# Sixteen filler-row transfers, placed behind the row loads of the third turn of tiles in place of in front of them

## The reference

```
probs = softmax(xf @ gate_w.T)                 # 4096 tokens, 16 experts
top_w, top_idx = top_k(probs, 4)               # 4 experts for each token, weights scaled to sum 1
act  = silu(xf @ w1[e].T) * (xf @ w3[e].T)     # hidden size 128
moe_out = sum over the token's 4 experts of weight * (act @ w2[e].T)
x = layernorm(x + moe_out + shared(x))
```

## Time and profile before

| | |
|---|---|
| median of 3 runs | 611.17 us |
| lowest, highest | 606.96, 620.32 us |
| the profiled execution | 603.63 us |
| its span (first to last instruction) | 601.8 us |
| PE, DVE, ACT, POOL busy | 86%, 75%, 61%, 58% of the span |
| first row load of the second half | 303.56 us |
| the sixteen pads on SP | 318.86 to 336.0 us |
| mean granted TensorE clock | 0.95 of full speed |

### The profile page before, as it was taken

The page is one execution under the profiler, slowest core; times in us unless marked ns, Lnnn a source line. Parts: engine busy times, 40 slices in busy tenths (PEclk is TensorE's granted clock), DMA queues, the critical chain, the costliest instruction groups (busy, mean ns, idle before and its releaser), DMA issues.

```text
span 601.8 us, 11085 instructions
## 1 busy us (share of the span) xinstructions
PE 518.6 (86%) x3184; PEld 450.2 (75%) x3184; DVE 448.6 (75%) x1053; ACT 369.8 (61%) x844; POOL 346.3 (58%) x320
## 2 busy tenths in 40 slices
PE   5997999999998999887597789989898999889752
PEld 2786878787877878775466688889897888888641
DVE  5868899999899989998896434444456877867544
ACT  4735585868586858751653445666575676775535
POOL 0331223868687786757788556565656666657520
PEclk9998999999999999998789589899999999999778
DMA  7999645978596857579967655555559998987873
GB/s 244 200 224 341 92 115 118 286 206 209 132 207 172 162 180 172 134 180 298 325 190 226 177 177 152 150 174 157 164 170 295 312 315 277 324 287 270 277 281 138
DMA packets 79006, 128.07 MB, mean 213 GB/s; under 512 B 10358, under 2 KB 57911, under 8 KB 78650
## 3 DMA queue, kind: packets, MB, share of 16 engines
q1 hardware_dynamic: 42714, 61.21, 36.3%
q0 software_dynamic: 28688, 58.35, 34.6%
q10 hardware_dynamic: 7552, 7.88, 3.8%
HBM read 75.89 MB, written 47.35 MB: 205 GB/s over the span
## 4 chain that ended last, share of the span: by engine, by line
PE 43%; DVE 25%; ACT 10%; issue 9%; another core or an unknown queue 5%; DMA 3%; SPq 3%; POOL 2%; ACTq 0%; DVEq 0%; POOLq 0%
PE bank L811 6%; PE bank L1028 6%; PE bank L1030 6%; PE bank L1029 5%; PE bank L833 4%; PE bank L1077 4%; PE bank L865 3%; PE bank L947 2%; ACT ty L1310 2%; SPq L535 2%; DVE x1c L1426 2%; PE bank L985 2%; DVE vc L1426 2%; ACT xtT_hi L1295 2%
## 5 line engine op out<-in xcount | busy, mean ns | idle before, releaser
L778 POOL DMA_INDIRECT token_parts<-ty,goes x144 | 141.0, 979 | 94.6 <-issue 32.7
L749 POOL DMA_INDIRECT expert_rows<-row,slot x112 | 128.8, 1150 | 60.9 <-issue 33.9
L1028 PE MATMUL bank<-w_hi,xtT_hi 128*128 x288 | 89.7, 311 | 9.2 <-DVE xtT_lo L1785 7.3
L1029 PE MATMUL bank<-w_lo,xtT_hi 128*128 x288 | 84.0, 292 | 1.6 <-issue 1.6
L1030 PE MATMUL bank<-w_hi,xtT_lo 128*128 x288 | 82.7, 287 | 0.7 <-issue 0.7
L1785 DVE TENSOR_TENSOR xtT_lo<-bank,xtT_hi 128x512 fp32r<-128x512 f32 x72 | 49.5, 688 | 23.7 <-issue 12.1
L1028 PEld LDWEIGHTS bank<-w_hi,xtT_hi 128*128 128x128 f32 x288 | 56.6, 197 | 13.7 <-issue 13.4
L1770 DVE TENSOR_TENSOR taT_lo<-bank,taT_hi 128x256 fp32r<-128x256 f32 x72 | 30.3, 420 | 47.0 <-issue 23.8
L1310 ACT ACTIVATE ty<-bank,tail 128x256 f32<-128x256 f32 x144 | 62.0, 495 | 0.0
L1288 ACT ACTIVATE tsl<-bank 128x256 f32<-128x256 f32 x72 | 29.4, 408 | 51.3 <-remote 34.9
L1295 ACT CAST xtT_hi<-bank 128x512 fp32r<-128x512 f32 x72 | 43.4, 602 | 24.9 <-remote 16.0
(11 more groups left out here) (229 smaller groups left out, 1342.2 us busy)
## 6 DMA issues: line engine op xcount, KB each, us to landing
xt<-expert_rows SPq DMA_DIRECT2D x144, 129.0 KB
row<-token_parts SPq DMA_DIRECT2D x18, 640.0 KB
xT<-in_xT SPq DMA_DIRECT2D x8, 512.0 KB
xtok<-in_b_out SPq DMA_DIRECT2D x8, 512.0 KB
xtok<-in_x POOLq DMA_DIRECT2D x8, 512.0 KB
x<-taps POOLq DMA_DIRECT2D x8, 512.0 KB
x<-ups POOLq DMA_DIRECT2D x8, 512.0 KB
w_hi<-in_w POOLq DMA_DIRECT2D x1, 4096.0 KB, 16.9
```

Source lines behind the costliest of these rows:

```text
L749: pool.indirect_dma_start(out=rows_d, out_offset=bass.IndirectOffsetOnAxis(ap=slot[q][:, n:n + 1], axis=0), in_=src[:, n // TOPK, n % TOPK ...
L778: pool.indirect_dma_start(out=parts_d, out_offset=bass.IndirectOffsetOnAxis(ap=goes[:, q_ * UNROLL + u:q_ * UNROLL + u + 1].bitcast(U32), ...
L1028: te_.matmul(ps, x_hi, w_hi, start=first, stop=False)
L1029: te_.matmul(ps, x_hi, w_lo, start=False, stop=False)
```

## The change

In `between`, the call of `pads()` moves from after the turn with number 1 to after the turn with number 2. Nothing is added or removed.

```diff
             def between(g):
-                if g == 1:
+                if g == 2:
                     pads()
-                if g == 2:
                     table_row(1)
                 if g == TFULL - 1:
```

## The result

The changed kernel takes **617.87 us** as the median of 6 runs (615.0 to 626.83), beside 610.7 us for the kernel before in 6 runs (606.96 to 620.32). By medians that is 7.2 us more; the ratio is 1.0161 with a 95% interval of 1.0114 to 1.0208, or 9.8 us. So the change made the kernel slower, by 1.2% in the medians and 1.6% in the ratio. The forecast, 607.4 us, has the wrong sign, and the time lies 0.9 us above the upper end of the range.

What follows compares the result with a forecast made beforehand. SP's loads standing behind the pads were taken as the bound, with PE's pace after pair 12. The hole moves to pair 12 and shrinks 3.8 us: 603.6 to 599.8 profiled, plus 7.5 gives a 607.4 us median; range 602 to 617.

Steps and rivals of the forecast that it cites:

- The case that the effect is absorbed later: Rival, chance 0.10: a later wait that does not move absorbs the gain; the time stays at 611.2 us.
- the halt moves with the pads: Main case, chance 0.42: PE's and ACT's halt follows the pads; pair 12 at 352.7, a gain of 3.8 us.
- tail copied at 328.5: Main case's time for pair 7's tail copy, with pair 7's transposes at 327.15; pair 11's loads issued by 329.5.
- The text's own sign: ACT's long wait before a silu: 330 to 347 if the halt moves with the pads, 324 to 332 if it stays.
- the halt stays and the hole grows: Rival, chance 0.32: halt not tied to the pads; pair 12 at 356.5 to 361.7, loss 0 to 5.2 us, 613.8 us.
- block with its register loads: SP's sixteen pads with two register loads: bounds 12.9 us (pads 0.70 us apart) and 18.01 us (as profiled before).
- table and register load: On SP, the table transfers and the register load behind them, up to the first row load: 1.94 us.
- load to transposes: From SP's issue of the first row load to PE's transposes, including the landing of 2.57 us: 3.28 us.
- The threshold of this rival: The loss decides once SP issues the block later than 333.3; that needs pair 7's tail copied after 332.3.
- the costs at nothing: Pad writes beside POOL's scatters, and the wait for `padded` behind the fourth turn (2.57 us if uncovered), were put at nothing.
- The rival without a halt: Rival, chance 0.12: pads run 0.70 us apart, block 12.9 us, pair 12 at 347.6; 8.9 us less, 602.3 us.
- theory A: From the experiments: the halt stays between pairs 7 and 8, delaying pair 7's tail copy and everything behind pair 11's loads.

Runs made afterwards that it cites:

- fit_b: Pads dealt out on SP: five behind pair 5's loads, one each behind 6's and 7's, nine behind 9's; 618.59 us, ratio 0.9942 to the kernel before.
- e_first: All sixteen pads behind pair 3's loads, on the chip without halts; 559.5 us, ratio 0.9998 to the kernel before.
- e_after_again: The changed order (sixteen pads behind pair 11's loads) built again, on the chip without halts; 560.56 us, ratio 1.0013 to the kernel before.
- before_again: The kernel before, unchanged, run again on a second chip with halts; 618.54 us, ratio 1.0046 to the kernel before.
- a hold of PE: PE repeats the transposes of pair 6's first tile forty times; 630.3 us in the kernel before, 627.46 us in the changed kernel.

## Why the prediction was wrong

**What bounds the kernel: right.** A loss ahead of pair 12 reached the end one to one (9.1 us at pair 12, 9.0 at the last pair), at the forecast pace of 3.3 us a pair. The case that the effect is absorbed later did not come.

**The step that failed: the choice between the two cases.** The prediction put two terms side by side, with pair 12 at 352.7 or at 356.5 to 361.7, and chose the first, "the halt moves with the pads". The reason given was the coincidence, the 8.58 us lying inside the block and the other waits of the kind being at most 4.8 us. In the changed kernel PE halts between pair 7 and pair 8 with no pad issued. On the clock of before, ACT's long wait is at 333.0 to 339.6 and the first pad at 342.4. So the term "tail copied at 328.5" became 340.6, and pair 12 came at 365.6 instead of 352.7. The text's own sign, ACT's long wait between 330 and 347 for the first case and at 324 to 332 for the second, would have named the wrong case: the wait had moved to a later silu, but not with the pads. What did go with the pads is the 8.58 us at the one silu, as the profiles above show. A coincidence in one trace weighed more than it could bear: the four shorter waits without pads had already shown that pads are not needed. The Trainium skill (Runtime: NRT & Kernel Launch, section Instruction fetch mechanics) had been read as favouring the case that came: a fetch belongs to a place in the program. The traces agree with that only in part: PE's long step stayed between pair 7 and pair 8, but ACT's long wait changed its instruction, and in `fit_b` the step is one pair earlier. Its "mostly hidden" would not agree with halts of 8 us, if fetches are their cause, which stays open (below).

**The rival "the halt stays and the hole grows": right in its mechanism, too small in two terms.** Its own working, on the clock of the profile before (the one after less 5.8 us):

| term | predicted | measured |
|---|---|---|
| pair 7's tail copied | 337.4 | 346.41 - 5.8 = 340.6 |
| pair 11's loads done | 338.4 | 347.46 - 5.8 = 341.7 |
| block with its register loads | 12.9 to 18.01 | 347.46 to 367.27 = 19.81 |
| table and register load | 1.94 | 367.27 to 369.23 = 1.96 |
| load to transposes | 3.28 | 369.23 to 371.42 = 2.19 |
| pair 12's transposes | 356.5 to 361.7 | 365.6 |

The tail copy is 3.2 us later than I took it, the block 1.8 us longer than its upper bound, the landing 1.1 us shorter: 3.9 us above the upper end, 361.7. The first error is "as now": pair 7's copy was taken to stay where the one old profile had it, +17.4 us behind pair 5, and it lies at +20.6 to +20.8 in all three profiles of the change. That is not scatter of the changed kernel: on ACT the halt comes later there. The second is that one slow block (18.01) was taken as the worst case; with halts the sixteen pads alone, without their register loads, took 15.34 to 20.69 us in eleven profiles. The threshold of this rival, "the block is issued later than 333.3", counts from the first register load, and was crossed by 8.4 us (347.46 - 5.8 = 341.7).

**Terms that held:** the order on SP, the table's 1.94 us, the costs at nothing (pair 16's loads, behind the wait for `padded`, were issued at 374.4, right behind pair 12's tail copy at 373.3; and the pairs behind 12 keep their pace).

**The rival without a halt** (pads at 0.70 us each) came true on the other chip in its size of the block, 12.8 us with its register loads (328.55 to 341.37) against 12.9, and not in its gain: 1.0013. By theory A the hole, a block of 12 us less what the buffers cover, is then the same in front of 8 and of 12 (the old order has no profile there). The 8.9 us were a comparison of a kernel without a halt with one that has it, which is not what the change does.

**The range** ended at 617, since the rival's upper end, 616.4, was taken from one halt and one block. Either of the two errors above, 3.2 us or 1.8 us, added to it would have held the time, 617.87.

## What to carry to other kernels

A block of transfers on one queue costs little where it is issued while its consumer is held up by something else. Before moving it, ask what hid it, and whether that stays. When loads in front of the block wait for a buffer, the block starts when that buffer comes free, so a delay of the consumer is passed on to everything behind: a place just ahead of such a wait (behind pair 10) can be cheap where the one just behind it (behind pair 11) is not. And when two things coincide in one trace, look for either alone elsewhere in the same trace before tying them together.

## What the runs showed of the hardware that I had not expected

**Chips differ by 50 us, in halts.** The same kernel before took 560.3 us on one chip and 611 to 619 on the four others; the profiles show mean granted clocks of 0.956 to 0.968 there and 0.935 to 0.953 on the others. From pair 5 to the last pair it is 193 to 195 us on the first (186 in `e_first`, whose block lies ahead of pair 5) and 231 to 247 on the others. The profiles show the difference as stretches in which PE, ACT and SP go on at 0.7 us an instruction or stand still ("issue", "remote"). The instruction queue carries the same on both. Its row of the page in `e_after_again`, which has no halts, is that of before:

```profile
q8 instruction: 26, 0.43, 0.3%
```

Equal number and bytes on this queue speak against more fetches; slower ones, or another cause outside the kernel, were not told apart. What a halt waits for stays open, and so does why a hold of PE swallowed it.

**After a wait PE ran at half its clock, and the loss has a tail.** Windows of the changed kernel (from:to, length, PE busy, granted clock, DMA share, GB/s): while it waits for pair 12, behind it, and then.

```profile
360.00:371.40 11.40, 0.36 (x4) 0.73 0.54 156
371.40:375.30 3.90, 3.88 (x17) 0.50 0.74 206
375.50:385.00 9.50, 9.50 (x85) 1.00 0.59 171
```

Behind 11.06 us of idling PE was granted 0.50, the lower of its two levels (1.2 GHz), for 3.9 us. Products that come 0.12 us apart at the full clock came 0.21 us apart. From pair 12 to pair 16 the changed kernel needs 13.2 us, the one before 11.6 (`before_again`, with a halt there, 16.7). So in the first two profiles 1.6 us are on top of the 9.1 at pair 16, most of which the scatter of the later pairs took back (9.0 at the end). On the chip without halts, a wait of 4.61 us had the same effect, a granted clock of 0.51 for the 3.2 us behind it.

**The issue of a pad** took 0.75 to 0.80 us on average (12.07 to 12.82 us for 16) where there are no halts, against about 0.5 us for a row load; with halts 0.96 to 1.29 us.
